# Constant sums in four 32-column tiles, and sixteen 32-row products in ordered rounds, in a gated cross-attention and feed-forward kernel

## The reference

```python
scores = jnp.einsum('bhdn,bhen->bhde', qh, kh) * scale
attn = jax.nn.softmax(scores, axis=-1)
out = jnp.einsum('bhde,bhen->bhdn', attn, vh)      # vh = k * wv + bv
x = x + jnp.tanh(g_xattn[0]) * (2.0 * (att_global + att_local) * wp + bp)
x = x + jnp.tanh(g_ffn[0]) * _L0_ffn_ref(_layernorm(x, axis=-1), ...)   # int8-like, gelu, 2048 hidden
```

## Time and profile before

| | |
|---|---|
| median of 3 runs | 394.27 us (394.17 to 396.25) |
| the profiled execution | 394.15 us, its span 392.3 us |
| outside the span | 1.85 us |
| PE busy | 365.2 us, 93% of the span |
| DVE busy | 320.3 us, 82% |
| ACT busy | 259.2 us, 66% |
| POOL busy | 105.5 us, 27% |
| matmul time of lines 1069 and 1100 | 111.9 and 110.0 us |

### The profile page before, as it was taken

One profiled execution on the slowest core, in us unless ns is written; L12 is line 12 of the kernel. 1 busy time (PEld: TensorE's weight loads), 2 busy tenths in 40 slices (PEclk: granted clock), 3 DMA queues, 4 the chain that ended last, 5 costly groups with the idle time before them and its releaser, 6 DMA issues.

```text
span 392.3 us, 5890 instructions
## 1 busy us (share of the span) xinstructions
PE 365.2 (93%) x2087; PEld 218.0 (56%) x2110; DVE 320.3 (82%) x599; ACT 259.2 (66%) x474; POOL 105.5 (27%) x169
## 2 busy tenths in 40 slices
PE   6779899999997797999999999999999999999995
PEld 4657787687685675454455455455544444444442
DVE  3289999999999877999999989978598876686653
ACT  1578877877874450789959988788899997620000
POOL 2653855855845661039200000000000000000000
PEclk9699999999999698999999999999999999999999
DMA  7999987843232550467767760000499999920123
GB/s 223 321 376 382 388 304 281 270 176 100 100 109 67 201 162 3 186 254 297 301 248 305 304 250 0 3 0 2 179 390 402 424 427 423 340 119 28 81 109 107
DMA packets 14528, 84.74 MB, mean 216 GB/s; under 512 B 1889, under 2 KB 2145, under 8 KB 5026
## 3 DMA queue, kind: packets, MB, share of 16 engines
q1 hardware_dynamic: 13840, 83.89, 56.3%
q10 hardware_dynamic: 658, 0.46, 0.5%
HBM read 54.99 MB, written 29.36 MB: 215 GB/s over the span
## 4 chain that ended last, share of the span: by engine, by line
PE 80%; DVE 13%; issue 3%; DMA 2%; ACT 1%; POOL 1%; DVEq 0%; SPq 0%; POOLq 0%
PE PS L1069 28%; PE PS L1100 28%; PE PS L975 7%; PE PS L917 7%; DVE mxd L600 3%; PE PS L937 2%; PE PS L969 2%; PE PS L1031 2%; DVE mid L577 2%; DMA X<-in_x 2%; DVE ring L643 1%; PE PS L958 1%; DVE mid L586 1%; DVE hmax L615 1%; PE PS L948 1%
## 5 line engine op out<-in xcount | busy, mean ns | idle before, releaser
L513 ACT ACTIVATE ring<-PS,bias,sc 128x512 f32<-128x512 f32 x128 | 97.1, 782 | 30.3 <-PE PS L1069 17.3
L1069 PE MATMUL PS<-mid,w1q 128*128 128x512 bf16 x500 | 111.9, 382 | 1.8 <-DVE mid L787 1.3
L1100 PE MATMUL PS<-w2q,w1q 128*128 128x512 bf16 x501 | 110.0, 379 | 1.1 <-DVE w1q L869 0.6
L1100 PEld LDWEIGHTS PS<-w2q,w1q 128*128 128x128 bf16 x512 | 49.9, 98 | 60.9 <-issue 0.5
L1069 PEld LDWEIGHTS PS<-mid,w1q 128*128 128x128 bf16 x512 | 50.0, 98 | 60.7 <-issue 2.6
L800 DVE TENSOR_REDUCE hmax<-ring 128x1 f32<-128x2048 f32 x30 | 67.5, 2278 | 5.4 <-ACT ring L513 5.4
L532 ACT ACTIVATE ring<-ring,sc 128x2048 f32<-128x2048 f32 x30 | 57.6, 1990 | 7.2 <-DMA ring<-spilled_hidden 7.2
L860 DVE TENSOR_SCALAR w1q<-ring 128x2048 bf16<-128x2048 f32 x30 | 36.6, 1223 | 22.8 <-PE PS L1100 18.7
L917 PE MATMUL PS<-ring 128*128 128x129 f32 x256 | 32.0, 286 | 1.4 <-ACT ring L454 1.4
L975 PEld LDWEIGHTS PS<-w2q,ring 128*128 128x128 f32 x256 | 29.2, 192 | 6.1 <-issue 6.1
L917 PEld LDWEIGHTS PS<-ring 128*128 128x128 f32 x256 | 31.2, 202 | 1.7 <-issue 1.7
(11 more groups left out here) (108 smaller groups left out, 405.6 us busy)
## 6 DMA issues: line engine op xcount, KB each, us to landing
spilled_hidden<-ring SPq DMA_DIRECT2D x20, 1024.0 KB, 3.9
ring<-spilled_hidden SPq DMA_DIRECT2D x20, 1024.0 KB, 8.9
ring<-in_ctx SPq DMA_DIRECT2D x8, 1024.0 KB, 10.0
ring<-in_ctxT SPq DMA_DIRECT2D x8, 1024.0 KB, 5.3
X<-in_x SPq DMA_DIRECT2D x7, 1024.0 KB, 12.8
out<-X SPq DMA_DIRECT2D x7, 1024.0 KB, 10.5
ring<-in_w1T SPq DMA_DIRECT2D x4, 1024.0 KB, 10.4
ring<-in_w2T SPq DMA_DIRECT2D x8, 512.0 KB, 3.8
```

The lines of the kernel that those rows point to most:

```text
L513: nc.scalar.activation(ring[:, s * CH + c, (h % CH) * N:(h % CH + 1) * N], PS[:, hidden_bank(s, h), :], ACT.Gelu, scale=S1, bias=bias1[:, ...
L1069: mm = nc.tensor.matmul(PS[:, hidden_bank(s, h), :], w1v[:, k, h * P:(h + 1) * P], xqT[:, s, k, :], start=(k == 0), stop=(k == NH - 1))
L1100: mm = nc.tensor.matmul(PS[:, par * NT + i, :], hq[:, c, k, i * P:(i + 1) * P], w2v[:, kk, :], start=(kk == 0), stop=(kk == KH - 1))
```

## The change

The constant row of head h is now computed only in the partitions 32h to 32h + 31 (a stationary operand of 32 columns), all heads in the same 128 columns of PSUM. So `c_sb`, `bpt` and `psC` shrink from 512 to 128 columns, and the row of head h is there only in the row group h. Each output bank therefore needs four products, one per head, with 32 rows and 128 columns each: 16 in place of 4. They go in four rounds; in round n bank i takes head (i + n) % 4, so that the four products of a round use different row groups and different banks. A new semaphore, `cr_done`, is raised by each product, and PE waits at the head of the rounds 1 to 3 until all products of the rounds before are complete.

```diff
-        c_sb = cut(D)
+        c_sb = cut(P)
-        bpt = mid[:, 1536:2048]
+        bpt = mid[:, 1536:1536 + P]
-        psC = PS[:, 7, :]
+        psC = PS[:, 7, 0:P]
...
-            nc.scalar.activation(bpt, psC, ACT.Copy, scale=tg[:, 0:1]).then_inc(scaled, 1)
+            for h in range(NH):
+                nc.scalar.activation(bpt[32 * h:32 * h + 32, :], PS[32 * h:32 * h + 32, 7, h * P:(h + 1) * P], ACT.Copy,
+                                     scale=tg[32 * h:32 * h + 32, 0:1]).then_inc(scaled, 1)
...
             def constant_sums(b):
...
-                for h in range(NH):
-                    for g in range(2):
-                        mm = nc.tensor.matmul(psC[:, h * P:(h + 1) * P], bvb[:, NH * g + h, :], Tn_sb[:, NH * g + h, :],
-                                              start=(g == 0), stop=(g == 1))
+                for g in range(2):
+                    for h in range(NH):
+                        mm = nc.tensor.matmul(psC[32 * h:32 * h + 32, :], bvb[:, NH * g + h, 0:32],
+                                              Tn_sb[:, NH * g + h, :], start=(g == 0), stop=(g == 1))
...
             def value_product(b):
...
-                for i in range(NT):
-                    nc.tensor.matmul(PS[:, OUT_BANK[i], :], first_row[32 * i:32 * i + 32, :], c_sb[32 * i:32 * i + 32, :],
-                                     start=True, stop=False)
+                for n in range(NH):
+                    if n > 0:
+                        pe.wait_ge(cr_done, 16 * b + 4 * n)
+                    for i in range(NT):
+                        h = (i + n) % NH
+                        nc.tensor.matmul(PS[:, OUT_BANK[i], h * P:(h + 1) * P], first_row[32 * h:32 * h + 32, :],
+                                         c_sb[32 * h:32 * h + 32, :], start=(n == 0), stop=False).then_inc(cr_done, 1)
```

More of the change, by code:

```diff
@@ L174, in gated_xattn_ffn @@
             ("rz_done", "rw_done", "en_done", "t_done", "tn_done", "tl_done"))
-        m_done, c_done, row_done = (sem(n) for n in ("m_done", "c_done", "row_done"))
+        m_done, c_done, row_done, cr_done = (sem(n) for n in ("m_done", "c_done", "row_done", "cr_done"))
         o_done, x2_done, nm_done, sq_done, mxd_done = (sem(n) for n in
@@ L645, in constant_row @@
             def constant_row(b):
-                dve.wait_ge(scaled, 2 * NH + 3)
+                dve.wait_ge(scaled, 3 * NH + 2)
                 dve.wait_ge(c_done, b + 1)
@@ L953, in constant_sums @@
                 pe.wait_ge(tn_done, 2 * b + 2)
-                pe.wait_ge(scaled, 2 * NH + 3)
+                pe.wait_ge(scaled, 3 * NH + 2)
                 wait(pe, x2_done, 4 * b)
-                for h in range(NH):
-                    for g in range(2):
-                        mm = nc.tensor.matmul(psC[:, h * P:(h + 1) * P], bvb[:, NH * g + h, :], Tn_sb[:, NH * g + h, :],
-                                              start=(g == 0), stop=(g == 1))
+                for g in range(2):
+                    for h in range(NH):
+                        mm = nc.tensor.matmul(psC[32 * h:32 * h + 32, :], bvb[:, NH * g + h, 0:32],
+                                              Tn_sb[:, NH * g + h, :], start=(g == 0), stop=(g == 1))
                 mm.then_inc(c_done, 1)
```

## The result

The changed kernel takes 411.85 us (median of 4, 410.77 to 413.03) against 394.38 us: ratio 1.0432, 95% interval 1.0385 to 1.048, slower by 17.5 us. The forecast was slower, 405.4 us, range 400 to 416. The time is in the range, but 6.4 us above the forecast; the case that came true is the first rival, "the clock falls in most turns", which had a chance of 0.25 and stood at about 413. A few disturbed executions in later comparisons are left out of their ratios.

The account below looks back on a forecast made before the run. PE was taken to bound the kernel, with four fifths of the chain. Turn 0 +0.48, turns 1 to 5 +5.95, turn 6 +0.86, turn 7 +1.85 and turn 6's clock +2.1 made +11.2 on 394.15: 405.4 us, range 400 to 416.

Parts of the forecast that it names:

- first rival: Longer idle time before line 937 lets the clock fall in most turns: 409 to 420 us, about 413, chance 0.25.
- How line 969 ran, and that nothing hides it: Line 969's four row groups run side by side, 0.94 us on the path; added time moves the whole turn.
- The price of a round: Line 969's new rounds: R, one round with its wait for completion, is 0.62 us, between 0.30 and 1.0.
- 3R - 0.67: General form of the time added to each of turns 1 to 5, R being one round; +1.19 us forecast.
- The term that was left out of the sum: Serialised semaphore increments of concurrent tiles: some 0.08 us more per round, about 2 us in total.
- Turns 1 to 5, +5.95: Rounds ahead of line 975 add 1.19 us in each of five ordinary turns; shorter constant sums save nothing there.
- Turn 0, +0.48: Shorter sums start the row earlier, but rounds delay line 975's first load from 35.20 to 35.68.
- Column tiles side by side: Line 958's sums in four column tiles run concurrently, four passes deep: some 0.75 us instead of 2.05 in turn 0.
- serial case: Column tiles of line 958 do not run side by side, so its sums stay as long: 403.3 us, chance 0.10.
- Turn 6, +0.86 and +2.1 for the clock: Rounds delay line 975 by 0.86 us; idle time of 3.7 us before line 937 brings a clock fall, +2.1.
- Turn 7, +1.85: Line 975 loads 0.75 us earlier, but 24 of its passes may run at 1.2 GHz, +2.6; sum +1.85.
- Faster: Hand-over and loads of the rounds hidden in the queue, R below 0.32: over 2 us faster, chance 0.07.

Follow-up runs that it names:

- e1: The changed kernel with six warming products added behind the constant sums in each turn, filling PE's idle time: 406.54 us, ratio 1.0303.
- e8: The changed kernel with six warming products behind the constant sums and one semaphore increment per round instead of four: ratio 1.0282.
- e7: The kernel before with its constant sums cut to one product of 512 columns, local branch and three heads' biases left out: 396.45 us, ratio 1.0055.
- e5: The changed kernel with six warming products and each bank's products from one row group without waits, three heads' rows left out: 392.94 us, ratio 0.9956.
- e9: The changed kernel with two rounds of 256 columns, one wait, and six warming products behind the constant sums: 397.63 us, ratio 1.0089.
- e10: The changed kernel with three warming products behind the constant sums in each turn: 408.65 us, ratio 1.041.
- e4: The changed kernel with two rounds of 256 columns, two heads in each 64-column tile, one wait instead of three: 402.07 us, ratio 1.0198.
- e2: The changed kernel with each bank's four products from one row group, without waits, three heads' rows left out: 401.39 us, ratio 1.0174.
- e3: The changed kernel with one semaphore increment per round, on its last product, instead of four: 414.62 us, ratio 1.052.

## Why the prediction was right and where it was off

The span grew by 18.6 us in the profiled execution. By stretches between the first loads of the sums: up to turn 1 +2.1, turns 1 to 5 +13.7, turn 6 +1.7, the rest +1.0.

The time lies in the range, but that is in part luck. The prediction named as a sign of being wrong a clock "that falls in every turn", and that is what happened: the case on which 405.4 us stood is out. The range held the time because it took in half of the first rival.

*How line 969 ran, and that nothing hides it*: right. The turn grows by what the path from `key_rows` to the value products grows.

*The price of a round*: right in mechanism, a little small. R was 0.67 for 0.62, and a turn at 2.4 GHz 1.35 us longer (e1) for 1.19; the prediction's own 3R - 0.67 gives 1.34 with the R measured. The term that was left out of the sum is there: e8 against e1 shows 0.07 us a round for the four increments in place of one. The Trainium skill (TensorE: Matmul & The Clock Gate, "The cost: per-tile semaphore tail") gave 0.08 by its 26 ns each; the traces agree.

*Turns 1 to 5, +5.95*: here the step failed, and it failed in the clock. The prediction let the clock fall in turn 6 and turn 7 only and held the ordinary turns safe, because the stretch from 117.0 to 120.8 had kept 2.4 GHz across a hole of 2.38 us. The hole of 2.53 us in each ordinary turn did not keep it: five turns cost 13.7 us, of which 5 x 1.35 = 6.8 are the waits and 7.0 the clock, 1.4 a turn. One stretch that held was too little to rest on; in e7 a hole of 2.61 us held in three turns and failed in two.

How much is the hole's and how much the rounds' shows in the turns 1 to 5 of the profiled executions, by the idle time of PE's loads ahead of line 937 (939) in the turns 2 to 5:

| kernel | idle time, us | waits in a turn | turns with a fall |
|---|---|---|---|
| before | 1.04 | 0 | 0 of 5 |
| e1, e8 | 0.92 | 3 | 1 of 5, 0 of 5 |
| e5 | 0.92 | 0 | 0 of 5 |
| e9 | 0.47 | 1 | 0 of 5 |
| e10 | 1.59 | 3 | 4 of 5 |
| e4 | 2.05 | 1 | 3 of 5 |
| e2, e7 | 2.53, 2.61 | 0 | 3 of 5, 2 of 5 |
| changed, e3 | 2.53 | 3 | 5 of 5, 5 of 5 |

With a hole of about 2.5 us and no waits half of the turns fell; with the waits behind it all ten did. So both have a part, and how much of the 1.4 us is the rounds' stays open. Open as well is whether the warming products help by shortening the idle time or by the work that they add: no run parts the two.

*The first rival*: it named the case, but its 413 us is luck. It reckoned with three to five falls at 3 us each, and with `gram` losing time. There were falls in all eight turns, each ordinary one cost 1.4 us, and `gram` (line 919) took 3.59 us as before. A fall did cost about 3 us where it came earlier in the rounds (turn 1 of e1, turn 2 of e10). Its sum is not clean either: three to five falls at 3 us in place of the one at 2.1 give 412 to 418 us, not 409 to 420.

*Turn 0, +0.48*: 0.8 us up to the value products' first load (36.19 for 35.20, with 0.2 us of it from ahead of the turn), then a fall that was not forecast, 1.15 us.

*Column tiles side by side*: right, 0.64 us forecast 0.75. This is what made the hole. The serial case is out.

*Turn 6, +0.86 and +2.1 for the clock*: the fall came (PEclk line). The idle time of the loads grew to 3.8 us where 3.7 was forecast, but not in one piece: line 909, a single product that waits for DVE, parts it into 1.01 and 2.77 us. Up to the first `add_product` behind its value products (line 664, now 666) turn 6 took 13.32 us in place of 9.56, +3.8 where 3.0 was forecast. Yet the whole turn grew by 1.7 us only: 2.0 us came back behind that point, which the prediction did not have; see the last section.

*Turn 7, +1.85*: right. From the first load of the sums to that of the value products it took 5.07 us in place of 5.63, -0.6 for the -0.75 forecast, though the sums, forecast at 1.2 GHz, ran at 2.4. Line 981 took 6.20 us in place of 3.78, +2.4 for +2.6, most of it at 1.2 GHz. What is behind line 981, which the prediction left untouched, got 0.8 us shorter; why is not shown.

*Faster*: out. The wait is not hidden in the queue; it decides at R = 0.40, and R is 0.67. With the waits gone and the hole filled (e5) the form costs nothing, but it is then another computation.

## What to carry to other kernels

Work of TensorE that lies in a gap is not free to remove. Here 1.4 us a turn of useful but uncritical products went; behind the longer gap the clock fell, in some turns by the gap alone (e7) and in every turn with the waits behind it, and that cost as much again as the waits. Before shortening something off the path, look at the length of the idle time that results and at stretches at 1.2 GHz behind such gaps, and be wary of a single one that held. A wait of TensorE for its own products cost the whole latency of load, passes and hand-over (here 0.67 us against 0.22 us of streaming), so that rounds should be few and wide (0.43 us a turn for two in place of 1.35 for four).

## What the runs showed of the hardware that was not expected

VectorE slows down beside GpSimd. In turn 6 the eight scalings of 128 by 128 (line 643, 645 after) are the same in both kernels. Before:

```profile
L643 DVE TENSOR_SCALAR ring<-ring,rw x8: 273/667/1073, 127.2 to 131.7; 128x128 f32<-128x128 f32 x8
```

After:

```profile
L645 DVE TENSOR_SCALAR ring<-ring,rw x8: 270/272/1161, 147.4 to 149.6; 128x128 f32<-128x128 f32 x8
```

The median is 667 ns in one and 272 ns in the other (minimum/median/maximum in the rows), 4.78 us for the eight against 2.52. Before, GpSimd's quantising of the weights (lines 364 and 366) ran beside all of them; in the changed kernel, whose attention came later, GpSimd was through after the first. In the kernel before every other scaling takes about 1.06 us and ends within 0.1 us of the end of a GpSimd operation, and the one behind it is short. This line gave 2.3 us back to turn 6; line 642 just ahead of it, also beside GpSimd, took 0.6 us of that away again (0.76 us for 0.17). It was seen in these two traces and not tested by a run of its own. The Trainium skill (SBUF — State Buffer, "Who interferes with whom") describes a port pair that VectorE and GpSimd share and lock for a whole instruction; the rows fit that.
